# Both expert layers by Strassen's scheme: seven block products for each 2x2 blocks, with sums by VectorE and in PSUM

## The chip, the cores and the metric

One core of a Trainium2 chip runs one program. The metric is the device time of one execution in microseconds (us); three executions are shown as their median. A profiled execution gives the trace on which everything below rests. TensorE (PE; its weight loads are PEld) does matrix products into PSUM, eight banks of 512 float32 a partition; VectorE (DVE), ScalarE (ACT) and GpSimd (POOL) do element-wise work; SyncE (SP) starts most DMAs.

## The reference

Input x is 4 samples x 512 tokens x 256 channels. Two layers of a transformer-like network are computed: modulated attention over heads and a Mamba block, a modulated linear layer and an fp8 linear layer, embeddings with layer norms, attention with 16 heads, and last the part that matters here:

```python
x = x + _L1_ffn_ref(_L1_cond2_ref(x, cond_512, ...), ...)

# _L1_ffn_ref, with xf = x.reshape(-1, 256), E = 8 experts of 512 hidden units
logits = xf @ gate_w.T + gate_b        # RMS-normed, softmax, top-1 value g
norm_g = g / (g + 1e-6)
h = gelu(einsum('nd,edh->neh', xf, w1) + b1)     # exact gelu
y = einsum('neh,ehd->ned', h, w2) + b2
out = (y * norm_g[:, None, None]).sum(axis=1)    # over all eight experts
```

Every token goes through all eight experts, so the experts together are one two-layer network 256 -> 4096 -> 256 in float32.

## The kernel before

The program is one function, `program`, with one instruction stream an engine (`block.tensor`, `block.scalar`, `block.vector`, `block.gpsimd`, `block.sync`), and semaphores between them. Activations lie transposed: channels on the 128 partitions (C = 2 chunks), a sample's 512 tokens along the free dimension. The order on each engine is the order of the code; nothing is planned at run time. The stages follow each other: first attention and Mamba until about 680 us, the linear and embedding layers until about 1000, attention until 1190, and the stage in question from there.

The lead-in (from line 1331): `decoded(b)` computes each sample's 256x256 decoder weights (line 1339), VectorE copies them and the bias (2223, 2226). Between these stand the last steps of attention: `z_rows`, `zn_columns`, `attention_out` (1281) on TensorE, `normalise` (2189, 2191) and `attention_add` (2197) on VectorE. Then the products of line 1365 give y4, the network's input, for sample after sample; ScalarE adds the bias (1791). When all four are there TensorE does the gate: 32 products of 8 columns, 64 records, into bank 6 (1372), whose results VectorE (2235 to 2261) and ScalarE (1794 to 1798) turn into one factor a token.

The experts (`experts`, `hidden`): 4096 hidden units are FM = 32 blocks of 128. For block f of sample b TensorE does two products of 128x128 weights and 512 columns into one of four banks (`hidden`, 1381), ScalarE applies gelu into `hid` (1805), and two steps later TensorE adds two products of that block with w2 into the two banks of the sample's output (1396), which stay open for all 32 blocks:

```python
for f in range(FM + 2):
    if f < FM:
        hidden(b, f)
    ...
    if f >= 2:
        pe.wait_ge(s_hid, b * FM + f - 2 + 5)
```

Samples alternate between output banks 0, 1 and 6, 7 (`turn`). During sample 0 the gate factor is spread over the partitions in bank 7 (1406), four products a sample, and copied into `ngb` (2264). Samples 0 and 1 are written out; samples 2 and 3 are a loop. When a sample's last block is in, VectorE's `finish` adds b2 and multiplies by the factor (2269), adds to xT (2272), and SP sends the sample out (757). GpSimd does nothing in this stage. SP loads w1 and w2 during attention (semaphore s_ew).

## Time and profile before

| | us |
|---|---|
| median of 3 runs | 1680.3 |
| lowest, highest | 1673.84, 1683.36 |
| profiled execution, its own time | 1684.6 |
| its span in the trace | 1682.8 |
| TensorE busy | 1507.3 |
| VectorE busy | 836.5 |
| ScalarE busy | 805.5 |
| GpSimd busy | 477.2 |
| mean granted TensorE clock | 0.949 of 2.4 GHz |

How to read it: the span goes from the first to the last instruction of the trace. A group of instructions is written "line engine op out<-in shapes xcount | busy us, mean ns of one | idle us before it, and what ended most of it". One float32 product stands as two records of weight load and two of matmul; a matmul record's duration contains the passage through the array, so successive records overlap and their spacing, not their duration, is the pace. A timeline line is "start us, length in us, engine, line, operation, xcount [idle before <- what ended it]". A window line gives the window, its length, the busy time and count for PE, PEld, DVE, ACT and POOL, then the granted clock as a share of 2.4 GHz, the DMA share and GB/s.

### The profile page before, as it was taken

How to read it: one execution, taken by the hardware profiler on the slowest of the kernel's cores; microseconds unless marked ns; L12 is line 12 of the kernel's file. 1: busy time of each engine (PE TensorE's matmuls, PEld its weight loads, DVE VectorE, ACT ScalarE, POOL GpSimd, SP SyncE). 2: the span in 40 equal slices, each digit the busy share in tenths (PEclk: the TensorE clock that was granted, in tenths of full speed). 3: DMA queues.
4: the chain of work that ended last, by engine and by line, in shares of the span. 5: the costliest groups of instructions: out<-in, count | busy, mean ns of one | idle time of the engine just before them, and what ended most of it. 6: DMA issues, size and time to landing. Idle time of an engine off the chain costs nothing.

```text
span 1682.8 us, 18326 instructions
## 1 busy us (share of the span) xinstructions
PE 1507.3 (90%) x6640; PEld 848.9 (50%) x6652; DVE 836.5 (50%) x868; ACT 805.5 (48%) x1346; POOL 477.2 (28%) x140
## 2 busy tenths in 40 slices
PE   5888796699999998979998968898999999999998
PEld 3666342488888887534443323332454444444443
DVE  6994676499797978744335656674100000000000
ACT  2432476499797977513331756776311121221121
POOL 0997300099797977003213200000000000000000
PEclk7899899699999999889999989999889999999999
DMA  6100011213222113110121261220000000000000
GB/s 255 63 16 1 0 51 78 113 52 125 90 110 78 51 46 136 36 39 19 57 75 49 88 244 39 57 56 1 1 0 0 1 13 0 13 0 0 13 0 13
DMA packets 35604, 87.47 MB, mean 52 GB/s; under 512 B 8238, under 2 KB 24836, under 8 KB 32836
## 3 DMA queue, kind: packets, MB, share of 16 engines
q1 hardware_dynamic: 35524, 86.39, 15.1%
q8 instruction: 51, 0.84, 0.2%
q14 instruction: 29, 0.24, 0.0%
HBM read 68.10 MB, written 18.21 MB: 51 GB/s over the span
## 4 chain that ended last, share of the span: by engine, by line
PE 55%; ACT 3%; issue 2%; DVE 2%; DMA 1%; DVEq 1%; ACTq 0%
PE ps L1381 13%; PE ps L1396 13%; PE ps L1256 3%; PE ps L1123 3%; PE ps L1298 3%; PE ps L1244 2%; PE ps L1149 2%; PE ps L1085 2%; ACT arena L1765 1%; PE ps L955 1%; DMA arena<-mrow 1%; PE ps L549 1%; PE ps L1281 1%; PE ps L1007 1%; PE ps L1157 1%
## 5 line engine op out<-in xcount | busy, mean ns | idle before, releaser
L2309 POOL TENSOR_TENSOR arena<-arena 128x2048 f32<-128x2048 f32 x63 | 287.3, 4586 | 167.6 <-DVE arena L1953 167.4
L1953 DVE TENSOR_TENSOR_SCAN arena<-arena,ps 128x1024 f32<-128x1024 f32 x128 | 284.2, 2271 | 45.0 <-ACT arena L1608 22.4
L1805 ACT ACTIVATE arena<-ps,arena 128x512 f32<-128x512 f32 x128 | 87.9, 687 | 348.7 <-PE ps L1381 348.7
L1381 PE MATMUL ps<-arena 128*128 128x512 f32 x512 | 241.7, 597 | 0.0
L1396 PE MATMUL ps<-arena 128*128 128x512 f32 x512 | 239.3, 592 | 0.0
L1765 ACT ACTIVATE arena<-ps,rho 128x512 f32<-128x512 f32 x256 | 158.6, 687 | 60.6 <-PE ps L1298 59.6
L1608 ACT ACTIVATE arena<-arena,mam 128x511 f32<-128x511 f32 x256 | 165.9, 709 | 34.4 <-DVE arena L1953 34.4
L2185 DVE TENSOR_REDUCE mxs<-ps 128x1 f32<-128x512 f32 x224 | 141.7, 684 | 61.7 <-PE ps L1244 59.8
L2269 DVE SCALAR_TENSOR_TENSOR arena<-ps,b2s,arena 128x512 f32<-128x512 f32 x8 | 5.6, 746 | 334.4 <-PE ps L1396 334.4
L1381 PEld LDWEIGHTS ps<-arena 128*128 128x128 f32 x512 | 97.9, 192 | 121.4 <-issue 121.2
L1396 PEld LDWEIGHTS ps<-arena 128*128 128x128 f32 x512 | 97.3, 190 | 122.4 <-issue 122.4
L943 PE MATMUL ps<-early,arena 128*128 128x128 f32 x768 | 129.7, 277 | 18.2 <-DVE arena L1953 17.9
L2289 POOL TENSOR_TENSOR arena<-arena 128x4096 f32<-128x4096 f32 x16 | 115.0, 7188 | 44.6 <-DVE arena L1872 44.6
L1596 ACT ACTIVATE arena<-arena,early 128x512 f32<-128x512 f32 x192 | 123.8, 708 | 0.1
L955 PE MATMUL ps<-early,arena 128*128 128x128 f32 x1024 | 121.5, 272 | 0.9 <-POOL arena L2309 0.8
L1298 PE MATMUL ps<-arena 97*128 97x512 bf16 x256 | 98.7, 394 | 18.2 <-DMA arena<-mrow 14.1
L955 PEld LDWEIGHTS ps<-early,arena 128*128 128x128 f32 x1024 | 113.6, 141 | 1.9 <-POOL arena L2309 1.2
L943 PEld LDWEIGHTS ps<-early,arena 128*128 128x128 f32 x768 | 90.6, 142 | 31.8 <-DVE arena L1953 22.9
L944 PE MATMUL ps<-arena 128*128 128x128 f32 x512 | 99.4, 276 | 0.0
L1244 PE MATMUL ps<-arena 96*128 96x512 bf16 x224 | 87.9, 392 | 0.0
L806 PE MATMUL ps<-early,arena 128*128 128x128 f32 x512 | 64.6, 288 | 21.3 <-POOL arena L2289 21.2
L1256 PE MATMUL ps<-arena 128*32 128x512 f32 x512 | 68.5, 607 | 13.2 <-ACT arena L1765 13.2
(311 smaller groups left out, 1868.8 us busy)
## 6 DMA issues: line engine op xcount, KB each, us to landing
arena<-bc_scratch SPq DMA_DIRECT2D x32, 512.0 KB, 3.7
batch_scratch<-arena SPq DMA_DIRECT2D x2, 3072.0 KB, 9.1
arena<-batch_scratch SPq DMA_DIRECT2D x6, 1024.0 KB, 7.1
arena<-q_scratch SPq DMA_DIRECT2D x96, 64.0 KB, 2.1
arena<-k_scratch SPq DMA_DIRECT2D x96, 64.0 KB, 2.1
arena<-in_dec_w SPq DMA_DIRECT2D x1, 3855.0 KB, 16.6
arena<-in_cond SPq DMA_DIRECT2D x1, 3739.5 KB, 11.7
arena<-in_ids SPq DMA_DIRECT2D x4, 768.0 KB, 7.1
```

What stands on the lines that cost most here:

```text
L943: pe.transpose(ps[:, FEED + m, t * P:(t + 1) * P], dub[:, k % 2, t, m * P:(m + 1) * P], ident)
L955: last = pe.matmul(ps[:, t, m * P:(m + 1) * P], state[:, k % SLOTS, m, t * P:(t + 1) * P], ident, start=False, stop=(k % NS == NS - 1 and ...
L1244: pe.matmul(ps[:, (hg + s) % 3, :], q[0:STACK, i, qc * P:(qc + 1) * P], k[0:STACK, i, :], start=True, stop=True).then_inc(s_s_mm, 1)
L1298: pe.matmul(ps[:, 3 + (hg + n) % 3, :], k[0:STACK + 1, i, kc * P:(kc + 1) * P], q[0:STACK + 1, i, :], start=True, stop=True).then_inc(s_t_ ...
L1381: last = pe.matmul(ps[:, 2 + f % 4, :], w1[:, c, f * P:(f + 1) * P], y4[:, b if isinstance(b, int) else bass.ds(b, 1), c, :], start=(c == ...
L1396: last = pe.matmul(ps[:, 6 * turn + o, :], w2[:, f - 2, o * P:(o + 1) * P], hid[:, (f - 2) % 4, :], start=(f == 2), stop=(f == FM + 1))
L1596: act.activation(dub[:, k % 2, t, :], duT[b % 2][:, t, :], ACT.Copy, scale=bt[:, b, t, n:n + 1])
L1608: last = act.activation(decay[:, (2 * k + h) % 3, i, 1:S], dt[b % 2][:, m, 1:S], ACT.Exp, scale=a_neg[:, m * NS + n:m * NS + n + 1])
L1765: act.activation(pt[:, j % 4, i], ps[:, 3 + (hg + n) % 3, :], ACT.Exp, scale=rho[:, 0:1]).then_inc(s_pt, 1)
L1953: dve.tensor_tensor_scan(half, view(decay[:, (2 * k + h) % 3], [[1, 2 * S]]), view(ps[:, FEED + 2 * h, :], [[1, 2 * S]]), 0.0, ALU.mult, A ...
L2185: dve.tensor_reduce(mxs[:, hg % 2, qc, i:i + 1], ps[:, (turn + s) % 3, :], AX, ALU.max).then_inc(s_max, 1)
L2309: pool.tensor_tensor(state[:, k % SLOTS], state[:, k % SLOTS], view(c_rows[:, j % 2, k % G, :], [[0, M], [1, S]]), ALU.mult).then_inc(s_hc, 1)
```

## The change

The hidden layer takes w1 as 2x2 blocks: rows by chunk k of the input, columns by half of the hidden units (16 blocks of 128 each). A sample's y4 is 2x2: chunk by half of the tokens. The four quarters of the hidden layer's output are made from seven block products instead of eight (the form with shared partial sums, after Winograd). The second layer does the same with w2 (half of the hidden units by output chunk) and the quarters of the hidden activations. The weight sums (`w1_s1`, `w1_s2`, `w1_s4`, the same for w2, and one difference written over each weight) are made once by VectorE before the stage, the sums of y4 once a sample (`x_sums`), the sums of the hidden quarters each round.

A round takes two hidden blocks of the lower and two of the upper half: 8 rounds a sample, 32 in all, all written out. TensorE's products have 256 columns. In a round, in this order: A1 (bank 4), B1 (bank 5), C1 (bank 6); three pairs of the second layer for the round before; A2, B2 (added into banks 4 and 5); two pairs of the second layer; B3, C2; two more pairs; two products a pair. ScalarE copies A1 (`first_in`) before A2 is added and applies gelu to the quarters h11, h22, h21, h12, two operations of 256 columns each. VectorE makes part2 (after B1), part3 and h22 (after B2), h21 (after B3), h12 (after C2), then t1, t2 (`t12`), a difference over h12, and t4 (`t34`): nine operations of 512 columns. The second layer's seven sums stay open in banks 0 to 3 for a sample; `quarters` joins them in the first round of the next sample, with eight operations of 256 columns, and `finish` follows in its second round. The gate products are spread over round 0 between the first layer's pairs, into bank 7; the gate's VectorE and ScalarE steps over rounds 1 to 3; the spreading of the factor goes to round 5 of each sample and its copy to round 6. Storage moves to freed places (the decoded weights, t sums and `first_in` into `mam`, the quarters into `hT`, `part2`, `part3`, `ngb`, `moe` into `early` and `diag`).

The diff, cut to its core:

```diff
@@ block.tensor @@
+            def pair(bank, n, weights, x, first, last):
+                b, r = divmod(n, ROUNDS)
+                for i in range(2):
+                    f = 2 * r + i
+                    done = pe.matmul(ps[:, bank, i * S // 2:(i + 1) * S // 2], weights[:, f, :], x,
+                                     start=first and i == 0, stop=last and i == 1, skip_group_check=True)
+                return done
...
+            def both(bank, half, n, weights, x):
+                r = n % ROUNDS
+                for i in range(2):
+                    f = 2 * r + i
+                    done = pe.matmul(ps[:, bank, half * S // 2:(half + 1) * S // 2], weights[:, f, :], x[:, i, :],
+                                     start=(r == 0 and half == 0 and i == 0),
+                                     stop=(r == ROUNDS - 1 and i == 1 and (half == 1 or bank == 1)))
+                return done
...
+            def second(n, chunk):
+                h11, h12, h21, h22 = h_q[n % 2]
+                t1, t2, t4 = h_t[n % 2]
+                begins = n % ROUNDS == 0 and n
+                if chunk == 0:
+                    pe.wait_ge(s_hid, by_act(n, 4))
+                    if begins:
+                        pe.wait_ge(s_sums, at_vector["out0", n])
+                    both(0, 0, n, w2_b[0][0], h11)
+                    both(0, 1, n, w2_b[0][1], h21)
+                    last = both(1, 0, n, w2_s4, h22)
+                elif chunk == 1:
+                    pe.wait_ge(s_sums, at_vector["t12", n])
+                    both(2, 0, n, w2_s1, t1)
+                    last = both(2, 1, n, w2_s2, t2)
+                else:
+                    pe.wait_ge(s_sums, at_vector["t34", n])
+                    both(3, 0, n, w2_b[1][0], h12)
+                    last = both(3, 1, n, w2_b[1][1], t4)
+                last.then_inc(s_e_mm, 1)
...
+            pe.wait_ge(s_y4, B + 1)
+            pe.wait_ge(s_sums, 1)
+            for n in range(B * ROUNDS):
+                b, r = divmod(n, ROUNDS)
+                x11, x12, x21, x22 = (y4[:, b, k, j * S // 2:(j + 1) * S // 2] for k in range(C) for j in range(2))
+                t1, t2, t3, t4 = (y4_t[:, b % 2, j, :] for j in range(4))
+                if n:
+                    pe.wait_ge(s_hid, by_act(n - 1, 2))
+                pair(A_BANK, n, w1_b[0][0], x11, True, True).then_inc(s_h_mm, 1)
+                if n:
+                    pe.wait_ge(s_sums, at_vector["c21", n - 1])
+                pair(B_BANK, n, w1_s2, t2, True, True).then_inc(s_h_mm, 1)
+                if n:
+                    pe.wait_ge(s_sums, at_vector["c12", n - 1])
+                pair(C_BANK, n, w1_s1, t1, True, True).then_inc(s_h_mm, 1)
+                if n:
+                    second(n - 1, 0)
+                else:
+                    gates(0)
+                    gates(1)
+                pe.wait_ge(s_hid, by_act(n, 1))
+                pair(A_BANK, n, w1_b[0][1], x21, False, True).then_inc(s_h_mm, 1)
+                pe.wait_ge(s_sums, at_vector["u2", n])
+                pair(B_BANK, n, w1_b[1][0], t3, False, True).then_inc(s_h_mm, 1)
+                if n:
+                    second(n - 1, 1)
+                else:
+                    gates(2)
+                pe.wait_ge(s_sums, at_vector["u3", n])
+                pair(B_BANK, n, w1_b[1][1], t4, False, True).then_inc(s_h_mm, 1)
+                pe.wait_ge(s_sums, at_vector["c22", n])
+                pair(C_BANK, n, w1_s4, x22, False, True).then_inc(s_h_mm, 1)
+                if n:
+                    second(n - 1, 2)
+                else:
+                    gates(3).then_inc(s_gate_mm, 1)
+                if r == 5:
+                    spread_gates(b)
+            for chunk in range(3):
+                second(B * ROUNDS - 1, chunk)
@@ block.scalar @@
+            def gelu(quarter, src, n, upper):
+                r = n % ROUNDS
+                for i in range(2):
+                    f = upper * W_HALF + 2 * r + i
+                    last = act.activation(quarter[:, i, :], src[:, i, :], ACT.Gelu, bias=wf["b1"][:, f:f + 1])
+                last.then_inc(s_hid, 1)
+            for n in range(B * ROUNDS):
+                h11, h12, h21, h22 = h_q[n % 2]
+                act.wait_ge(s_h_mm, by_pe(n, 1))
+                if n:
+                    act.wait_ge(s_sums, at_vector["c21", n - 1])
+                act.activation(first_in, ps[:, A_BANK, :], ACT.Copy).then_inc(s_hid, 1)
+                if n == 1:
+                    act.wait_ge(s_ng, 1)
+                    act.activation(gs[:, 1, :], gs[:, 0, :], ACT.Ln, scale=1.0 / E, bias=eps32[:, 0:1])
+                    act.drain()
+                    act.activation(gs[:, 1, :], gs[:, 1, :], ACT.Exp, scale=-0.5).then_inc(s_gate_a, 1)
+                    act.preload_act_table_set("gelu_and_others")
+                if n == 2:
+                    act.wait_ge(s_ng, 2)
+                    act.activation(lg[:, :, :], lg[:, :, :], ACT.Exp, scale=2.0).then_inc(s_gate_a, 1)
+                    act.preload_act_table_set("gelu_and_others")
+                act.wait_ge(s_h_mm, by_pe(n, 4))
+                if n >= 2:
+                    act.wait_ge(s_e_mm, second_layer(n - 2, 3))
+                gelu(h11, view(ps[:, A_BANK, :], [[S // 2, 2], [1, S // 2]]), n, 0)
+                act.wait_ge(s_sums, at_vector["c22", n])
+                gelu(h22, h22, n, 1)
+                act.wait_ge(s_sums, at_vector["c21", n])
+                gelu(h21, h21, n, 1)
+                act.wait_ge(s_sums, at_vector["c12", n])
+                gelu(h12, h12, n, 0)
@@ block.vector @@
+            def weight_sum(out, a, b, op):
+                dve.drain()
+                dve.tensor_tensor(out, a, b, op)
+            def x_sums(b):
+                dve.wait_ge(s_y4, b + 2)
+                x11, x12, x21, x22 = (y4[:, b, k, j * S // 2:(j + 1) * S // 2] for k in range(C) for j in range(2))
+                t1, t2, t3, t4 = (y4_t[:, b % 2, j, :] for j in range(4))
+                dve.tensor_tensor(t1, x12, x11, ALU.subtract)
+                dve.tensor_tensor(t3, x22, x12, ALU.subtract)
+                dve.drain()
+                dve.tensor_tensor(t2, x22, t1, ALU.subtract)
+                dve.drain()
+                dve.tensor_tensor(t4, x21, t2, ALU.subtract).then_inc(s_sums, 1)
+            weight_sum(w1_s1, w1_b[1][0], w1_b[1][1], ALU.add)
+            weight_sum(w1_b[1][0], w1_b[0][0], w1_b[1][0], ALU.subtract)
             dve.wait_ge(s_wgt_mm, 1)
             dve.tensor_copy(dbias[:, :, :], ps[:, 4, 0:C * B])
             decoded(0)
             normalise(B * HG - 1, HG - 1)
             decoded(1)
             decoded(2)
+            weight_sum(w1_s2, w1_s1, w1_b[0][0], ALU.subtract)
             attention_add(B - 1, 0)
             decoded(3)
+            weight_sum(w1_s4, w1_b[0][1], w1_s2, ALU.subtract)
             attention_add(B - 1, 1)
+            weight_sum(w2_s1, w2_b[1][0], w2_b[1][1], ALU.add)
+            weight_sum(w2_b[1][0], w2_b[0][0], w2_b[1][0], ALU.subtract)
+            x_sums(0)
+            weight_sum(w2_s2, w2_s1, w2_b[0][0], ALU.subtract)
+            weight_sum(w2_s4, w2_b[0][1], w2_s2, ALU.subtract)
...
+            def quarters(n):
+                low, high = slice(0, S // 2), slice(S // 2, S)
+                dve.wait_ge(s_e_mm, second_layer(n - 1, 2))
+                dve.drain()
+                dve.tensor_copy(part2[:, low], ps[:, 0, low])
+                dve.drain()
+                dve.tensor_tensor(moe[0][:, low], part2[:, low], ps[:, 0, high], ALU.add)
+                dve.tensor_tensor(part2[:, high], part2[:, low], ps[:, 2, high], ALU.add)
+                dve.drain()
+                dve.tensor_tensor(part3[:, low], part2[:, high], ps[:, 2, low], ALU.add)
+                dve.drain()
+                out0 = dve.tensor_tensor(moe[0][:, high], part3[:, low], ps[:, 1, low], ALU.add)
+                out0.then_inc(s_sums, 1)
+                dve.wait_ge(s_e_mm, second_layer(n - 1, 3))
+                dve.tensor_tensor(part3[:, high], part2[:, high], ps[:, 3, low], ALU.add)
+                dve.drain()
+                dve.tensor_tensor(moe[1][:, low], part3[:, high], ps[:, 3, high], ALU.add)
+                dve.tensor_tensor(moe[1][:, high], part3[:, high], ps[:, 2, low], ALU.add).then_inc(s_sums, 1)
+            def finish(b):
+                dve.drain()
                 for o in range(C):
-                    dve.scalar_tensor_tensor(moe[:, o, :], ps[:, 6 * turn + o, :], b2s[:, o:o + 1], ngb[:, tok(b)],
-                                             ALU.add, ALU.mult)
-                dve.drain()
-                dve.tensor_tensor(xT[:, :, tok(b)], xT[:, :, tok(b)], moe, ALU.add).then_inc(s_x4, 1)
-                dve.drain()
-
-            dve.drain()
-            with dve.Fori(0, B // 2) as i:
-                finish(2 * i, 0)
-                finish(2 * i + 1, 1)
+                    dve.scalar_tensor_tensor(moe[o], moe[o], b2s[:, o:o + 1], ngb, ALU.add, ALU.mult)
+                dve.drain()
+                for o in range(C):
+                    last = dve.tensor_tensor(xT[:, o, tok(b)], xT[:, o, tok(b)], moe[o], ALU.add)
+                last.then_inc(s_x4, 1)
+            for n in range(B * ROUNDS):
+                b, r = divmod(n, ROUNDS)
+                h11, h12, h21, h22 = h_q[n % 2]
+                t1, t2, t4 = h_t[n % 2]
+                flat = lambda quarter: view(quarter, [[1, S]])
+                dve.wait_ge(s_h_mm, by_pe(n, 2))
+                dve.wait_ge(s_hid, by_act(n, 1))
+                dve.drain()
+                dve.tensor_tensor(part2, first_in, ps[:, B_BANK, :], ALU.add).then_inc(s_sums, 1)
+                if n == 1:
+                    gate_power()
+                if n == 2:
+                    gate_less_max()
+                if n == 3:
+                    gate_factor()
+                if r == 1 and b:
+                    finish(b - 1)
+                dve.wait_ge(s_h_mm, by_pe(n, 5))
+                dve.tensor_tensor(part3, first_in, ps[:, B_BANK, :], ALU.add).then_inc(s_sums, 1)
+                if n >= 2:
+                    dve.wait_ge(s_e_mm, second_layer(n - 2, 3))
+                dve.drain()
+                dve.tensor_tensor(flat(h22), part3, ps[:, C_BANK, :], ALU.add).then_inc(s_sums, 1)
+                if r == 4 and b < B - 1:
+                    x_sums(b + 1)
+                if r == 6:
+                    dve.wait_ge(s_ngb_mm, b + 1)
+                    dve.tensor_copy(ngb, ps[:, 7, :]).then_inc(s_ngb, 1)
+                dve.wait_ge(s_h_mm, by_pe(n, 6))
+                dve.tensor_tensor(flat(h21), first_in, ps[:, B_BANK, :], ALU.add).then_inc(s_sums, 1)
+                dve.wait_ge(s_h_mm, by_pe(n, 7))
+                dve.tensor_tensor(flat(h12), part2, ps[:, C_BANK, :], ALU.add).then_inc(s_sums, 1)
+                if r == 0 and b:
+                    quarters(n)
+                dve.wait_ge(s_hid, by_act(n, 5))
+                dve.tensor_tensor(flat(t1), flat(h12), flat(h11), ALU.subtract)
+                dve.drain()
+                dve.tensor_tensor(flat(t2), flat(h22), flat(t1), ALU.subtract).then_inc(s_sums, 1)
+                dve.tensor_tensor(flat(h12), flat(h22), flat(h12), ALU.subtract)
+                dve.drain()
+                dve.tensor_tensor(flat(t4), flat(h21), flat(t2), ALU.subtract).then_inc(s_sums, 1)
+            quarters(B * ROUNDS)
+            finish(B - 1)
```

## Rows read from the trace of the kernel before

**Rows 1.** The page's busy time by engine, whole span.
```profile
PE 1507.3 (90%) x6640; PEld 848.9 (50%) x6652; DVE 836.5 (50%) x868; ACT 805.5 (48%) x1346; POOL 477.2 (28%) x140
```

**Rows 2.** Groups of instructions by line from 1100 us on, expert stage.
```profile
L1381 PE MATMUL ps<-arena 128*128 128x512 f32 x512 | 241.7, 597 | 0.0
L1396 PE MATMUL ps<-arena 128*128 128x512 f32 x512 | 239.3, 592 | 0.0
...
L1805 ACT ACTIVATE arena<-ps,arena 128x512 f32<-128x512 f32 x128 | 87.9, 687 | 348.7 <-PE ps L1381 348.7
...
L1406 PE MATMUL ps<-early,gs 128*128 128x128 f32 x32 | 4.2, 275 | 0.0
```

**Rows 3.** Windows, with the granted clock.
```profile
1150.00:1180.00 30.00, 24.07 (x124) 7.32 (x125) 8.82 (x16) 20.44 (x35) 0.00 (x0) 1.00 0.00 1
1210.00:1230.00 20.00, 18.64 (x81) 13.99 (x79) 0.00 (x0) 3.79 (x6) 0.00 (x0) 0.79 0.00 1
1230.00:1250.00 20.00, 20.00 (x44) 9.23 (x45) 3.17 (x12) 6.24 (x10) 0.00 (x0) 0.87 0.00 0
1400.00:1500.00 100.00, 100.00 (x234) 44.28 (x233) 2.63 (x3) 20.36 (x30) 0.00 (x0) 1.00 0.02 6
```

**Rows 4.** Timeline from the decoder's bias to the first expert products.
```profile
1191.27 0.17 DVE L2226 COPY dbias<-ps 128x8 f32<-128x8 f32 x1 [5.26 <-PE ps L1339]
...
1204.11 0.69 DVE L2197 TENSOR_TENSOR xT<-ps,xT 128x512 f32<-128x512 f32 x1 [1.22 <-PE ps L1281]
...
1207.55 1.26 ACT L1791 ACTIVATE arena<-ps,dbias 128x512 f32<-128x512 f32 x2 [11.59 <-PE ps L1365]
...
1219.16 11.52 PEld L1372 LDWEIGHTS ps<-arena 128*128 128x128 f32 x64 [2.18 <-ACT arena L1791]
...
1230.63 7.69 PE L1381 MATMUL ps<-arena 128*128 128x512 f32 x12
...
1233.87 1.28 ACT L1799 ACT_TABLE_LOAD   x1
```

**Rows 5.** Timeline of TensorE, two like places of the expert stage, 64 blocks apart.
```profile
1442.58 1.88 PE L1381 MATMUL ps<-arena 128*128 128x512 f32 x4
...
1662.32 1.88 PE L1381 MATMUL ps<-arena 128*128 128x512 f32 x4
```

**Rows 6.** Timeline of the end.
```profile
1675.19 0.19 PEld L1396 LDWEIGHTS ps<-arena 128*128 128x128 f32 x1 [0.24 <-issue]
1676.37 1.41 DVE L2269 SCALAR_TENSOR_TENSOR arena<-ps,b2s,arena 128x512 f32<-128x512 f32 x2 [107.06 <-PE ps L1396]
1677.94 1.23 DVE L2272 TENSOR_TENSOR xT<-xT,arena 128x1024 f32 x1 [0.16 <-issue]
1679.34 0.57 SPq L757 DMA_DIRECT2D out<-xT  x1
```

**Rows 7.** Timeline of weight loads around the 256-column products of line 1157.
```profile
786.48 0.19 PEld L1157 LDWEIGHTS ps<-arena 128*128 128x128 f32 x1 [0.24 <-issue]
786.90 3.22 PEld L1157 LDWEIGHTS ps<-arena 128*128 128x128 f32 x15 [0.24 <-issue]
790.15 4.84 PEld L1085 LDWEIGHTS ps<-arena 128*128 128x128 bf16 x23
```

**Rows 8.** Groups by shape, whole span: the 128-column products of line 955.
```profile
L955 PE MATMUL ps<-early,arena 128*128 128x128 f32 x1024 | 121.5, 272 | 0.9 <-POOL arena L2309 0.8 <-DVE arena L2113 0.2
```

**Rows 9.** Groups by shape, whole span, VectorE.
```profile
L1926 DVE TENSOR_TENSOR arena<-arena 128x2048 f32<-128x2048 f32 x4 | 9.2, 2293 | 0.4
...
L2191 DVE TENSOR_TENSOR hT<-ps,zrec 128x256 f32<-128x256 f32 x16 | 6.8, 425 | 1.2
...
L1819 DVE TENSOR_TENSOR arena<-early 128x512 f32<-128x512 f32 x1 | 0.7, 693 | 4.0 <-DMA early<-in_early 4.0
```

**Rows 10.** Groups by shape, whole span, ScalarE on 256 columns.
```profile
L1494 ACT ACTIVATE arena<-arena 128x256 f32<-128x256 f32 x16 | 6.5, 409 | 5.5 <-DVE arena L1861 5.5
```

**Rows 11.** Timeline inside the attention stage: a product that waited for ScalarE.
```profile
1175.70 1.06 PE L1256 MATMUL ps<-arena 128*32 128x512 f32 x8 [1.14 <-ACT arena L1765]
```

More of the change, by code:

```diff
@@ L1367, in _, with gates @@
                 last.then_inc(s_y4_mm, 1)
-            pe.wait_ge(s_y4, B + 1)
-            for b in range(B):
+            def gates(b):
                 for t in range(TILES):
                     for c in range(C):
-                        last = pe.matmul(ps[:, 6, (b * TILES + t) * E:(b * TILES + t + 1) * E],
+                        last = pe.matmul(ps[:, 7, (b * TILES + t) * E:(b * TILES + t + 1) * E],
                                          y4[:, b, c, t * P:(t + 1) * P], gate_w[:, c, :],
@@ L1374, in _ @@
                                          start=(c == 0), stop=(c == C - 1))
-            last.then_inc(s_gate_mm, 1)
-            def hidden(b, f):
-                pe.wait_ge(s_hid, b * FM + f + 1)
-                for c in range(C):
-                    last = pe.matmul(ps[:, 2 + f % 4, :], w1[:, c, f * P:(f + 1) * P],
-                                     y4[:, b if isinstance(b, int) else bass.ds(b, 1), c, :],
-                                     start=(c == 0), stop=(c == C - 1))
-                last.then_inc(s_h_mm, 1)
@@ L1410, in _ @@
[L1410 to L1416 removed]
+                return last
+            def pair(bank, n, weights, x, first, last):
[5 more added lines that the diff above has]
+                return done
@@ new lines, in spread_gates @@
+            def spread_gates(b):
+                pe.wait_ge(s_ng, 3)
+                pe.wait_ge(s_ngb, b)
+                for t in range(TILES):
+                    col = b * TILES + t
+                    last = pe.matmul(ps[:, 7, t * P:(t + 1) * P], gs[:, 3, col:col + 1].to_broadcast([P, P]),
+                                     ident, start=True, stop=True)
+                last.then_inc(s_ngb_mm, 1)
+            pe.wait_ge(s_y4, B + 1)
[36 more added lines that the diff above has]
+                    spread_gates(b)
```

142 lines of the change are left out of this document (63 added, 79 removed).

## The prediction, before the change was built

> **What bounds the kernel now.** I began with the busy time by engine: TensorE works 90% of the span, VectorE and ScalarE about half of it [rows 1]. A share over the whole span says little of one stage, so I went to the groups by line. The two lines of the expert layers, 1381 and 1396, hold 481.0 us of TensorE's time with nothing idle before them, while ScalarE's gelu in the same stage works 87.9 us and waits 348.7 us for TensorE [rows 2]. Each product of 512 columns stands there as two records, so 1024 records are 512 products. The windows say the same of the middle of the stage: in 100 us TensorE is busy 100.00, VectorE 2.63, ScalarE 20.36, and the granted clock is 1.00, the 2.4 GHz level [rows 3]. The timeline gives the stage its ends: gate products from 1219.16, expert products from 1230.63 [rows 4]. In between all goes at one pace: two like places lie 219.74 us and 512 records apart, 0.4292 us a record [rows 5]. The last weight load is at 1675.19; its record takes the next slot and leaves it at 1676.05, and VectorE's closing sums start 0.32 us later [rows 6]. So the stage is 445.4 us of pure TensorE, of which 1024 x 0.4292 = 439.5 are the products; the other 5.9 are the gate-spreading products (4.2 us busy, [rows 2]) and a start at the lower clock. A change pays here exactly what it takes from TensorE's queue, as long as that queue never waits.
>
> **What is removed and added on TensorE.** Four samples of 32 blocks are worked as 32 rounds of four blocks. A round was 16 products of 512 columns, 32 records; it becomes 14 per layer, 28 products of 256 columns, 56 records. In columns that is 7/8. Whether time follows depends on the spacing at 256 columns. The expert stage has no such product, but line 1157 does, same types, other weights each time: weight loads from 786.90 to the first load of the next line at 790.15 make 3.25 us for 15, 0.2167 us a record, with loads of 0.19 us [rows 7]. The loads thus fit behind the product before. Sum: 1792 x 0.2167 = 388.3 us, against 439.5: **51.2 us saved**. The bounds: half of today's record, 0.2146, would give 384.6 (3.7 us better). At 128 columns line 955 takes 121.5 us for 1024 records, 0.1187 each [rows 8]; twice that, 0.2373, gives 425.2 (37 us worse). I take line 1157, the same width.
>
> The load is the thing to weigh: 0.19 of 0.2167 us is nearly the whole slot. The Trainium skill (TensorE: Matmul & The Clock Gate, Back-to-back issue gap) says that in a stream of load and matmul pairs both set the spacing, and that short matmuls come out slower than columns over clock, 81 against 56 ns at 128 columns. By that the halved width would lose part of its gain; by the record of line 955 that loss is small here, 0.1187 us where half of line 1157's record would be 0.1084.
>
> **Can the two other engines keep up?** VectorE goes from nothing to nine 512-column operations a round: 0.69 us each, from PSUM [rows 4] or SBUF [rows 9], 6.2 us, with gaps of 0.08 some 6.8. ScalarE does one copy (at most 0.69, the gelu of 512 columns [rows 2]) and eight gelus of 256 columns; the nearest row is 0.41 us [rows 10], say 0.45: 4.3 us. The round on TensorE is 56 x 0.2167 = 12.14 us, so neither is the bound by volume. What can bite is the order. I lay out a round from its first product, a pair of products being 0.87 us, a consumer starting 0.3 us after a slot ends (rounded from [rows 6]):
> A1 to 0.87, B1 to 1.73, C1 to 2.60, three second-layer pairs of the round before to 5.20, A2 to 6.07, B2 to 6.94, two pairs to 8.67, B3 to 9.54, C2 to 10.40, two pairs to 12.14.
> VectorE: part3 after B2, 7.24 to 7.93, c22 to 8.70. B3 needs the first at 8.67 and C2 the second at 9.54: 0.7 and 0.8 us spare, the tightest places. Then h21 to 10.53, h12 to 11.39. ScalarE is through h12 by about 12.3, the t sums follow to 13.8 and 15.3 (which is 3.1 into the next round). Of those the second layer needs t12 at 19.1 and t34 at 22.5, the gelus (11.4) at 14.7. The next part2 is then ready at 3.9, B2 wants it at 6.07. So in an ordinary round nothing waits. The x sums (four of 256 columns, 0.42 each by [rows 9]) and the spread factor's copy fall into the 1.1 us before B3's result or push h21 by 0.7 us, still 3 us early. I cost these at nothing; their cover is TensorE's own queue of second-layer pairs.
>
> **The three sample ends** are different. After h12 come eight adds and copies of 256 columns: out0 at 13.8 (needed at 14.7), out1 at 15.2, the t sums at 16.6 and 18.1, part2 of the next round at 18.8, where B2 wants it at 18.2: TensorE waits 0.7 us. Then two scaled sums and two adds of 512 columns (0.70 and 0.69 each, 3.0 us in all) stand before part3, which comes at 22.6 against B3's 21.5: 1.1 us more. That is 1.8 us, three times **5.4 us**; bounds nothing and twice that.
>
> **The start.** The weight sums, 2048 columns, 2.29 us each [rows 9], go into VectorE's gaps: two (4.6 us) before the bias copy, which had 5.26 us idle ahead of it; the third and fourth before the attention adds, of which the last moves from 1204.11 to some 1205.3, where the product that needs it is 8 us off; two more and the x sums until about 1213, since the first sample's y4 is ready at 1208.8; the last two until 1218. TensorE starts its first round at 1219.16 as before, when the last y4 is there [rows 4]: nothing. The 32 gate products (64 records, 11.5 us) stay, spread over round 0, where they cover the first waits. What moves is the clock: those 8-column products leave it at 0.79, and after them today's first twelve records take 7.69 us instead of 5.3, at the 1.2 GHz level [rows 3, 4]. Now round 0's 28 records (6.1 us) lie between gate products, so the lower clock can cost from 0 to 6.1 plus today's 2.5. I take 4.0, **1.5 us more**. The gate's ScalarE steps carry two table loads of 1.28 [rows 4] in each of two rounds, in the 4 us in which ScalarE waits for A2, and end before c22 is there; VectorE's gate steps (at most five of 0.3) follow part2 in rounds 1 to 3, from 3.9 to 5.4, before part3's 7.2: nothing. The samples are now all written out where two of four were a loop; the written-out first sample shows no idle time before its products either [rows 2], so nothing for fetching. The output transfers of samples 0 to 2 move a round back on SP, and nobody waits for them.
>
> **The end.** Now 3.1 us lie between the last slot and the output transfer's sums [rows 6]. Then: the first five of the output sums start under the last two pairs and end 0.9 us after the slot, three more take 1.3, the scaled sums and adds 3.0: 5.3 us, **2.2 more**. The transfer itself is the same size.
>
> **The sum**, against the profiled execution (span 1682.8, time 1684.6): -51.2 + 5.4 + 1.5 + 2.2 = -42.1, so 1642.5. The median shown is 1680.3, 4.3 below that execution, and the runs spread over 9.5; a new median should lie by it, so the forecast is **1638 us**. Over or under 0.5%, about 8 us, is what a measurement of this kernel can tell from no change.
>
> **The rivals.**
> *The loop slips in every round (chance 0.16).* The spare at B3 and C2 is 0.7 us; with slower semaphore hand-overs or gaps than I put, each round loses 0.6: 32 x 0.6 = 20 us, 1658. For: two tight places in each round, two dependent PSUM reads. Against: the gaps here come from rows.
> *Nothing waits (0.09).* Sample ends hidden, clock as today, spacing 0.2146: 3.7 + 5.4 + 1.5 = 10.6 off, 1628.
> *Weight loads show (0.05).* By the 128-column row, 37 us back: 1675, no change that can be told. For: 88% of the slot is load. Against: line 1157 runs exactly this. This is the way the Trainium skill's section on the issue gap, named above, would have it go.
> *Slower (0.05): the clock falls.* If TensorE's waits at B3 bring it to 1.2 GHz, a round costs up to 12.1 us more; from 42.1/12.1 = 3.5 such rounds on the gain is gone. If every round waits 0.8 us and then takes today's 2.5 us to recover, 3.3 x 32 = 106 us more: 1744. Against: in the attention stage TensorE waited 1.14 us for ScalarE, the window was only 80% busy, and the clock stayed at 1.00 [rows 3, 11].
> My own forecast has the remaining 0.65.
>
> **Numbers.** Forecast 1638; range 1628 to 1660, which takes in the first two rivals and the bounds of the sample ends and leaves out the last two (0.10) and some of the slipping loop. Faster by over 0.5%: 0.65 + 0.16 + 0.09 = 0.90; within: 0.05; slower: 0.05.
>
> **What would show it.** TensorE's weight loads in the expert stage 0.217 us apart; rounds 12.1 us long; the stage's end near 1632 in the trace; VectorE at about 55% there, ScalarE at 35%; waits of TensorE for VectorE only in rounds 8 and 9, 16 and 17, 24 and 25. Wrong would be: spacing above 0.225 with no wait named (loads), a wait before every B3 or C2 (loop), a granted clock below 0.95 from 1260 on (clock), VectorE's 512-column sums over 0.8 us.

## The result and the profile after

| | before | after |
|---|---|---|
| median, us | 1681.83 (4 runs) | 1635.14 (4 runs) |
| lowest, highest | 1673.84, 1685.69 | 1632.79, 1637.53 |
| profiled execution, its span | 1684.6, 1682.8 | 1633.2, 1631.4 |
| forecast | | 1638 (1628 to 1660) |

The measured ratio is 0.9728, with a 95% interval from 0.9688 to 0.9769. The medians differ by 46.7 us where 42.1 were forecast, the spans of the two profiled executions by 51.4. I read the new trace in the order of the forecast's steps. First the page's busy time by engine and the groups from 1180 us on (columns as in [rows 1, 2]):

```profile
PE 1454.8 (89%) x7408; PEld 994.1 (61%) x7420; DVE 1067.1 (65%) x1216; ACT 855.9 (52%) x1511; POOL 477.4 (29%) x140
```

```profile
L1412 PE MATMUL ps<-arena 128*128 128x256 f32 x896 | 215.5, 387 | 3.3 <-DVE early L2439 1.9 <-ACT arena L1870 1.4
...
L1421 PE MATMUL ps<-hT,arena 128*128 128x256 f32 x512 | 121.2, 380 | 0.0
...
L1421 PE MATMUL ps<-mam,arena 128*128 128x256 f32 x384 | 93.3, 379 | 0.0
L1878 ACT ACTIVATE hT<-hT,arena 128x256 f32<-128x256 f32 x192 | 85.7, 502 | 86.4 <-DVE hT L2443 54.9 <-DVE hT L2450 30.7 <-DVE hT L2452 0.8
...
L2456 DVE TENSOR_TENSOR mam<-hT 128x512 f32<-128x512 f32 x32 | 22.1, 692 | 28.9 <-ACT hT L1878 28.9
...
L2439 DVE TENSOR_TENSOR early<-mam,ps 128x512 f32<-128x512 f32 x32 | 22.0, 687 | 101.1 <-PE ps L1412 101.1
```

The 896 records of line 1412 and the 512 and 384 of line 1421 are the 1792 that were counted. With the 1024 of the kernel before [rows 2] they account for the whole difference in TensorE's number of records, 7408 against 6640 [rows 1]. VectorE's 512-column sums take 0.69 us, as priced. ScalarE's 256-column gelu takes 0.50 from SBUF where I had said 0.45; nothing follows from it, since ScalarE sits idle before it.

The windows, first the new trace's (columns as in [rows 3]), then two of the trace of before for the same times:

```profile
1180.00:1195.00 15.00, 13.14 (x68) 5.95 (x67) 9.67 (x13) 7.57 (x13) 0.00 (x0) 1.00 0.00 1
1195.00:1210.00 15.00, 14.11 (x35) 6.32 (x34) 14.43 (x13) 3.78 (x6) 0.00 (x0) 1.00 0.01 1
1210.00:1230.00 20.00, 18.64 (x88) 15.68 (x87) 4.51 (x6) 5.99 (x12) 0.00 (x0) 0.77 0.00 1
1230.00:1250.00 20.00, 20.00 (x80) 17.40 (x81) 9.70 (x17) 10.96 (x18) 0.00 (x0) 0.80 0.00 0
...
1300.00:1600.00 300.00, 298.09 (x1387) 260.82 (x1386) 168.38 (x264) 99.61 (x218) 0.00 (x0) 1.00 0.02 6
```

```profile
1180.00:1195.00 15.00, 13.14 (x70) 5.88 (x62) 2.90 (x9) 7.97 (x14) 0.00 (x0) 0.86 0.01 2
1195.00:1210.00 15.00, 15.00 (x33) 6.67 (x32) 2.77 (x5) 1.86 (x3) 0.00 (x0) 0.80 0.00 0
```

From 1300 to 1600 TensorE works 298.1 of 300 us at the 2.4 GHz level, VectorE 56%, ScalarE 33%: the forecast said 55 and 35. What TensorE misses there are the sample ends. They show in the timeline of weight loads, here the first of the three, with the ordinary round after it:

```profile
1332.49 2.56 PEld L1412 LDWEIGHTS ps<-arena 128*128 128x128 f32 x12
...
1338.93 0.73 PEld L1412 LDWEIGHTS ps<-arena 128*128 128x128 f32 x4 [0.42 <-DVE early L2429]
...
1342.40 1.59 PEld L1412 LDWEIGHTS ps<-arena 128*128 128x128 f32 x8 [1.02 <-DVE early L2439]
...
1345.75 2.56 PEld L1412 LDWEIGHTS ps<-arena 128*128 128x128 f32 x12
...
1357.84 2.56 PEld L1412 LDWEIGHTS ps<-arena 128*128 128x128 f32 x12
```

A round begins with twelve loads of line 1412 (A1, B1, C1). The ordinary one goes from 1345.75 to 1357.84, **12.09 us** (forecast 12.14), or 0.2159 a record. The one with the sample's end goes from 1332.49 to 1345.75, 13.26, so **1.17 us** more. The two waits that were named are the only ones, 0.42 us for line 2429 (part2) and 1.02 for 2439 (part3). Both lie in the next sample's second round; in its first, which the forecast's signs had allowed too, none shows.

The lead-in and the start, from the timeline; the last three lines are of the trace of before:

```profile
1189.35 0.17 DVE L2343 COPY dbias<-ps 128x8 f32<-128x8 f32 x1 [0.42 <-PE ps L1370]
...
1196.47 1.96 PE L1312 MATMUL ps<-hT,arena 128*128 128x512 f32 x4 [0.89 <-DVE xT L2297]
1213.51 2.46 PEld L1412 LDWEIGHTS ps<-arena 128*128 128x128 f32 x12 [2.19 <-ACT arena L1870]
...
1221.62 3.75 PEld L1402 LDWEIGHTS ps<-arena 128*128 128x128 f32 x16
...
1236.98 3.07 PEld L1421 LDWEIGHTS ps<-hT,arena 128*128 128x128 f32 x12
...
1237.41 3.05 PE L1421 MATMUL ps<-hT,arena 128*128 128x256 f32 x12
...
1240.30 1.89 PE L1412 MATMUL ps<-arena 128*128 128x256 f32 x8
```

```profile
1197.26 3.78 PE L1281 MATMUL ps<-hT,arena 128*128 128x512 f32 x4
...
1201.08 0.69 DVE L2197 TENSOR_TENSOR xT<-ps,xT 128x512 f32<-128x512 f32 x1 [3.02 <-PE ps L1281]
...
1238.16 1.88 PE L1396 MATMUL ps<-arena 128*128 128x512 f32 x4
```

And the end:

```profile
1621.86 0.84 PEld L1421 LDWEIGHTS ps<-mam,arena 128*128 128x128 f32 x4
...
1627.07 0.68 DVE L2418 TENSOR_TENSOR xT<-xT,diag 128x512 f32<-128x512 f32 x1
1627.93 0.57 SPq L788 DMA_DIRECT2D out<-xT  x1
```

The sum, step by step, against the forecast's; the stage is counted from the first product after y4 to the end of the span:

| step | forecast | profile | how |
|---|---|---|---|
| products | -51.2 | -52.6 | 1792 x 0.2159 = 386.9 against 439.5 |
| sample ends | +5.4 | +3.5 | 3 x 1.17 |
| start | +1.5 | +1.7 | see below |
| end | +2.2 | +1.7 | last slot 1622.94, last add ends 1627.75: 4.8 against 3.1 |
| sum | -42.1 | -45.7 | |
| stage, read directly | | -45.7 | 463.6 (1219.16 to 1682.8) to 417.9 (1213.51 to 1631.4) |
| ahead of the stage | 0 | -5.7 | 1219.16 to 1213.51 |

For the start I go by the starts of products. From 1213.51 to the first second-layer product of round 1, at 1237.41, are 23.9 us, and the lower clock costs another 0.3 behind that (those twelve records take 2.89 us, to 1240.30, where 12 x 0.2159 make 2.59). Less the 40 expert records in it (8.6) that is 15.6. Before, the gate products took from 1219.16 to 1230.63, 11.5 us, and the first twelve expert records from there to 1238.16, 7.5 where 12 x 0.4292 make 5.15, so 2.4 too long: 13.9 in all.

The last line was in no sum of the forecast. The windows show the granted clock at 1.00 from 1180 to 1210 where the trace of before has 0.86 and 0.80, and 3.7 of those 5.7 us lie between the bias copy and the first product after y4: 24.2 us (1189.35 to 1213.51) against 27.9 [rows 4]. The other 2.0 lie earlier and were not followed up. How far the 3.7 go by execution is looked at in experiment 8.

### The profile page after: what moved, and what is told of

Same layout as the page of the kernel before. It is cut to its first block, busy times and chain, and to the rows that moved or that the text cites. A ratio compares the mean times of both kernels' runs of the same rounds, so it can differ in the third digit from the quotient of the medians.

```text
span 1631.4 us, 20342 instructions
## 1 busy us (share of the span) xinstructions
PE 1454.8 (89%) x7408; PEld 994.1 (61%) x7420; DVE 1067.1 (65%) x1216; ACT 855.9 (52%) x1511; POOL 477.4 (29%) x140
## 3 DMA queue, kind: packets, MB, share of 16 engines
q1 hardware_dynamic: 35524, 86.39, 15.7%
## 4 chain that ended last, share of the span: by engine, by line
PE 53%; ACT 3%; DVE 2%; issue 2%; DMA 1%; DVEq 1%; ACTq 0%
PE ps L1412 12%; PE ps L1421 12%; PE ps L1287 4%; PE ps L1154 3%; PE ps L1329 3%; PE ps L1275 2%; PE ps L1180 2%; PE ps L1116 2%; ACT arena L1845 2%; PE ps L986 1%; DMA arena<-mrow 1%; PE ps L580 1%; PE ps L1312 1%; PE ps L1038 1%; PE ps L1188 1%
## 5 line engine op out<-in xcount | busy, mean ns | idle before, releaser
L1412 PE MATMUL ps<-arena 128*128 128x256 f32 x896 | 215.5, 387 | 3.3 <-DVE early L2439 1.9
L1412 PEld LDWEIGHTS ps<-arena 128*128 128x128 f32 x896 | 172.2, 193 | 30.0 <-DVE early L2439 3.1
L974 PE MATMUL ps<-early,arena 128*128 128x128 f32 x768 | 129.7, 277 | 18.3 <-DVE arena L2053 17.9
L1878 ACT ACTIVATE hT<-hT,arena 128x256 f32<-128x256 f32 x192 | 85.7, 502 | 86.4 <-DVE hT L2443 54.9
L986 PE MATMUL ps<-early,arena 128*128 128x128 f32 x1024 | 121.5, 272 | 0.9 <-POOL arena L2494 0.7
L1421 PE MATMUL ps<-hT,arena 128*128 128x256 f32 x512 | 121.2, 380 | 0.0
L1421 PEld LDWEIGHTS ps<-hT,arena 128*128 128x128 f32 x512 | 97.7, 191 | 13.4
L1878 ACT ACTIVATE hT<-ps,arena 128x256 f32<-128x256 f32 x64 | 26.9, 471 | 138.9 <-PE ps L1412 138.9
L1421 PE MATMUL ps<-mam,arena 128*128 128x256 f32 x384 | 93.3, 379 | 0.0
L2439 DVE TENSOR_TENSOR early<-mam,ps 128x512 f32<-128x512 f32 x32 | 22.0, 687 | 101.1 <-PE ps L1412 101.1
```

The lines of the kernel that those rows point to most:

```text
L974: pe.transpose(ps[:, FEED + m, t * P:(t + 1) * P], dub[:, k % 2, t, m * P:(m + 1) * P], ident)
L986: last = pe.matmul(ps[:, t, m * P:(m + 1) * P], state[:, k % SLOTS, m, t * P:(t + 1) * P], ident, start=False, stop=(k % NS == NS - 1 and ...
L1412: done = pe.matmul(ps[:, bank, i * S // 2:(i + 1) * S // 2], weights[:, f, :], x, start=first and i == 0, stop=last and i == 1, skip_group ...
L1421: done = pe.matmul(ps[:, bank, half * S // 2:(half + 1) * S // 2], weights[:, f, :], x[:, i, :], start=(r == 0 and half == 0 and i == 0), ...
```

## The experiments

The total of one kernel spreads over 5 to 21 us between executions, and goes with the mean granted clock (in experiment 2 from 1671.9 us at 0.959 to 1689.8 at 0.949). So I read each trace at the same places: **start**, from the first product after y4 to the first second-layer weight load of round 1, and **rest**, from there to the end of the span. The changed kernel has 23.5 and 394.4; 0.5 of the 394.4 is the lower clock, which reached into the first twelve loads (3.07 us for 2.56). The ratio beside each is against the kernel before, from runs on the same chip.

**1. 256 columns without the scheme.** The kernel before, each product in two halves.

```diff
-last = pe.matmul(ps[:, 2 + f % 4, :], w1[:, c, f * P:(f + 1) * P], y4[:, ..., c, :], ...)
+for h in range(2):
+    part = slice(h * S // 2, (h + 1) * S // 2)
+    last = pe.matmul(ps[:, 2 + f % 4, part], w1[:, c, f * P:(f + 1) * P], y4[:, ..., c, part], ...)
```
and the same for w2.

> The kernel before, with every expert product of 512 columns made as two of 256 (2048 records instead of 1024, no scheme). Theory (columns alone set the time, weight loads hide behind 256 columns): spacing 0.216 us a record, 2048 x 0.2159 = 442 against 439.5 us, so +3 us, no change that can be told. Rival (weight loads show at 256 columns, by the 128-column record of line 955): spacing 0.237, 486 us, +46 us.

Measured: ratio 1.0000 (0.9972 to 1.0029); the stage took 466.2 us (1211.25 to 1677.4), +2.6. Weight loads in mid-stage, from the timeline:

```profile
1501.27 1.70 PEld L1383 LDWEIGHTS ps<-arena 128*128 128x128 f32 x8
...
1508.17 1.70 PEld L1383 LDWEIGHTS ps<-arena 128*128 128x128 f32 x8
```

Between the two, 32 loads: 6.90 us, 0.2156 each. Doubling the number of loads and products costs 0.6% of the stage. The rival of 0.237 is out. This was the term on which most of the forecast hung, and it had come from 16 records of another stage [rows 7].

**2. Eight products in the changed kernel.**

```diff
+pair(A_BANK, n, w1_b[0][1], x21, False, False)
 pair(A_BANK, n, w1_b[0][1], x21, False, True).then_inc(s_h_mm, 1)
 ...
 both(3, 0, n, w2_b[1][0], h12)
+both(3, 0, n, w2_b[1][0], h12)
```

> The changed kernel with one pair of products more in each layer of each round, 32 products of 256 columns instead of 28, so as many columns as before the change, with all sums kept. It adds products, so its output is another. Theory (TensorE's queue is the round): 32 x 8 records x 0.2159 = +55 us on the changed kernel, about 1690, some 8 us slower than before the change. Rival (rounds are set by hand-overs between engines): part of the added products falls into waits, under +45 us.

Measured: 1679.4 us, ratio 0.9983 (0.9948 to 1.0019): the scheme with an eighth product is where the kernel before is. Rest 444.3, +49.9 on the changed kernel. The expectation was some 5 too high, and by my own reading: 252 added records lie in the rest, 54.4 us, but with longer rounds TensorE no longer waits at the sample ends (the trace has no wait of its loads for VectorE), which gives 3.5 back: 50.9. The 1690 also carried the changed kernel's long start (23.5), where this trace has 19.9; what else parts it from the median of 1679.4 one trace can't tell. The gain of the change is the missing product; that nothing else in it costs in an ordinary round, experiment 5 shows more directly.

**3 and 4. One or two more VectorE operations ahead of part3.**

```diff
 dve.wait_ge(s_h_mm, by_pe(n, 5))
+dve.tensor_tensor(part3, first_in, first_in, ALU.add)
+dve.drain()
```

> The changed kernel with one more VectorE operation of 512 columns (and its drain, 0.77 us) in each round ahead of part3. The trace of the changed kernel shows 0.57 us between the end of part3 and the weight load of B3. Theory (one tight place, priced by its own spare): 0.2 us late in each of 32 rounds, +6 us, with waits of B3's loads for VectorE. Rival (VectorE is 56% busy, so 0.77 us fits in a round of 12.1): +0.

> As the run before, with two more operations (1.54 us a round). Theory: 0.97 us late in each of 32 rounds, +31 us. Rival of free room by busy share: +0. Second rival (the waits bring TensorE's clock down to 1.2 GHz): over +100 us, granted clock below 0.95 in the stage.

Measured: one: ratio 0.9715 (0.9648 to 0.9782), rest 399.3, **+4.9**; two: 0.9895 (0.9841 to 0.9948), rest 423.0, **+28.6**. The waits of the first run (engine, line <- whom, us in total, times, longest) and two successive loads of its B3; then the same loads and the window of the second run:

```profile
PEld ps L1412 <- DVE early L2441: 11.6, 31, 1.8
```

```profile
1345.04 1.59 PEld L1412 LDWEIGHTS ps<-arena 128*128 128x128 f32 x8 [0.22 <-DVE early L2441]
...
1357.22 1.59 PEld L1412 LDWEIGHTS ps<-arena 128*128 128x128 f32 x8 [0.22 <-DVE early L2441]
```

```profile
1314.55 1.59 PEld L1412 LDWEIGHTS ps<-arena 128*128 128x128 f32 x8 [0.99 <-DVE early L2443]
...
1317.90 2.56 PEld L1412 LDWEIGHTS ps<-arena 128*128 128x128 f32 x12
...
1327.49 1.59 PEld L1412 LDWEIGHTS ps<-arena 128*128 128x128 f32 x8 [0.99 <-DVE early L2443]
```

```profile
1300.00:1600.00 300.00, 281.41 (x1285) 239.91 (x1285) 191.05 (x297) 93.23 (x205) 0.00 (x0) 1.00 0.02 6
```

With one more sum an ordinary round is 12.18 us (1345.04 to 1357.22), +0.09; with two it is 12.94 (1314.55 to 1327.49), +0.85. In the changed kernel VectorE is idle for 5.3 us of a round (44% of 12.09), and yet 1.54 more cost 29 us: the spare that counts is the one at that place. The rule by busy share fails. The second rival fails as well: the loads of B3 wait 1 us in each round, TensorE is idle for 6% of the window, and the clock stays at 1.00, which was read before from the attention stage [rows 11] and now holds here.

**5. The sums nearly taken away.**

```diff
-dve.tensor_tensor(part2, first_in, ps[:, B_BANK, :], ALU.add).then_inc(s_sums, 1)
+dve.tensor_tensor(part2[:, some], first_in[:, some], ps[:, B_BANK, some], ALU.add).then_inc(s_sums, 1)
```
with `some` the first 64 columns, and so for all nine.

> The changed kernel with VectorE's nine sums of each round made on 64 of 512 columns, the rest left out (so its output is another); products, gelus and order as they are. Theory (the sums are hidden but for the three sample ends, where TensorE waits some 1.2 us each): -3.5 us. Rival (sums cost something in every round): -10 us or more.

Measured: ratio 0.9689 (0.9655 to 0.9723), rest 390.4, **-4.0**; the trace has no wait of the loads for VectorE. So all 32 x 9 sums together cost the changed kernel 3.5 us (the other 0.5 is the clock in the changed kernel's rest), and that is the price of its three sample ends, 3 x 1.17. Its start took 15.7 us, with the granted clock at 1.00 throughout, though its round 0 has the same products in the same order:

```profile
1207.81 2.46 PEld L1412 LDWEIGHTS ps<-arena 128*128 128x128 f32 x12 [2.19 <-ACT arena L1870]
...
1215.59 1.97 PEld L1402 LDWEIGHTS ps<-arena 128*128 128x128 f32 x16
...
1223.48 2.56 PEld L1421 LDWEIGHTS ps<-hT,arena 128*128 128x128 f32 x12
...
1223.69 2.75 PE L1421 MATMUL ps<-hT,arena 128*128 128x256 f32 x12
```

Sixteen loads for the gate take 1.97 us here; at the lower level they had taken 3.75. The short sums are not the reason for the full clock, as far as the totals can tell: the profiled execution took 1615.6 us at a mean clock of 0.961, the other six 1629.1 to 1632.7 at 0.947 to 0.950, about where the changed kernel lies.

**6. finish one round later.**

```diff
-if r == 1 and b:
+if r == 2 and b:
     finish(b - 1)
```

> The changed kernel with finish of a sample in the next sample's third round instead of its second, all else equal. Theory (of the 1.2 us that a sample end costs, 0.8 is B3 waiting for part3 behind finish): -2.3 us, the waits for line 2439 gone, those for part2 (0.4 us each) left. Rival (the wait only moves to the third round): 0.

Measured: ratio 0.9683 (0.9642 to 0.9724), rest 391.3, **-3.1**, of which 0.5 is again the lower clock in the other's rest: -2.6 for the -2.3 expected. The waits for part3 are gone, those for part2 left, 0.4 us each:

```profile
PEld ps L1412 <- DVE early L2429: 1.3, 3, 0.4
```

**7. The gate's products: all first, or one sample a round.** All ahead of round 0 (first diff), and, on top of 6, one sample in each of rounds 0 to 3 (second). Both diffs are cut: with the second the gate's ScalarE and VectorE steps move to rounds 4 to 6, the spreading of the factor to round 7 and its copy to the next sample's second round.

```diff
 pe.wait_ge(s_sums, 1)
+for b in range(B):
+    last = gates(b)
+last.then_inc(s_gate_mm, 1)
```
```diff
 if n:
     second(n - 1, 1)
-else:
-    gates(2)
+if n < B:
+    last = gates(n)
```

> The changed kernel with all 32 gate products ahead of round 0, as before the change. Theory (in round 0 they cover waits of TensorE for the two other engines, so that spreading them gives back what the clock costs): the 12.5 us that round 0 takes above its own columns become 11.5 for the gates, 3 of open waits and less time at the lower clock: +1 to +3 us. Rival (spreading them only lengthens the time at the lower clock): -2 to -5 us.

> As the run before, and the gate's 32 small products one sample each in rounds 0 to 3 instead of all in round 0, the gate's other steps in rounds 4 to 6, the spreading of the factor in round 7. Theory (the run of small products in round 0 holds TensorE at 1.2 GHz from about 1220 to 1237, which costs some 8 us): the granted clock stays at 1.00, the start is about 5.5 us shorter, -7.8 us on the changed kernel with the 2.3 of finish. Rival (the clock falls whatever the order): -2.3 us.

Measured, all first: ratio 0.9719 (0.9682 to 0.9755), start 21.7, rest 393.9. With no gate products in round 0 to cover it, TensorE's load for B3 waits 1.18 us for part3 there, once. The start lies between the starts that the changed kernel's own round 0 has had (15.7 to 24.0 with the next experiment), so this comparison is inconclusive.

One sample a round: ratio 0.9666 (0.9627 to 0.9706), median 1624.1 us against experiment 6's 1631.2, the stage 407.0 us against 417.9, the clock at 1.00 all through. But the profiled execution, at 1617.7, was the fastest of its six, and one of them took 1634.8. One profile at full clock could be luck, as in 5, so it was run again.

**8. Again, side by side.** The changed kernel; the version of 7 with two weight sums moved behind the attention adds; the kernel before.

```diff
-weight_sum(w1_s2, w1_s1, w1_b[0][0], ALU.subtract)
 attention_add(B - 1, 0)
 decoded(3)
-weight_sum(w1_s4, w1_b[0][1], w1_s2, ALU.subtract)
+weight_sum(w1_s2, w1_s1, w1_b[0][0], ALU.subtract)
 attention_add(B - 1, 1)
+weight_sum(w1_s4, w1_b[0][1], w1_s2, ALU.subtract)
```

> The changed kernel once more, beside the next run on the same chip. In five profiles with the changed kernel's round 0, the stretch from the first product of round 0 to round 1's second-layer pairs took between 15.7 and 23.7 us by how long the clock stood at its lower level. Theory (chance of each execution): it takes again something between 15.7 and 24, the rest of the stage, from there to the end of the span, 394 us as before. Rival (the length goes with the kernel's text): 23.5 us again.

> Gate products over rounds 0 to 3 and finish in the third round, as run before; and the third weight sum behind the first attention add, the fourth behind the second, where TensorE waited 0.9 us for that add in the trace of the changed kernel. Theory: granted clock 1.00 from round 0 on again; lead-in 0.9 us shorter when it runs at full clock; stage from round 0 to the end of the span 407 us; 7 to 9 us under the changed kernel's median. Rival (the full clock of that one profile was luck): the stage within 2 us of the changed kernel's less 2.5.

> The kernel before once more, for the clock in the lead-in: in its first trace the stretch from the bias copy to the first gate product took 27.9 us, in the changed kernel's 24.2. Theory (the clock there goes by execution, not by the change): the stretch lies anywhere from 24 to 28, the expert stage from the first gate product to the end of the span at 463.6 +-1. Rival (the change shortened it): 27.9 again.

Measured: the changed kernel 1632.03, ratio 0.9693 (0.9658 to 0.9727), start 24.0, rest 393.9, stage 417.9; the version 1622.64, ratio **0.9644** (0.9611 to 0.9676), stage 406.9. The windows of the version:

```profile
1195.00:1210.00 15.00, 15.00 (x32) 6.53 (x31) 9.83 (x8) 1.27 (x2) 0.00 (x0) 0.81 0.00 0
1210.00:1230.00 20.00, 18.64 (x78) 13.29 (x77) 13.50 (x15) 9.68 (x17) 0.00 (x0) 1.00 0.00 1
1230.00:1250.00 20.00, 20.00 (x109) 17.98 (x107) 8.91 (x14) 5.86 (x13) 0.00 (x0) 1.00 0.00 0
...
1300.00:1600.00 300.00, 299.96 (x1400) 263.41 (x1399) 172.37 (x270) 101.87 (x223) 0.00 (x0) 1.00 0.02 6
```

and the changed kernel's again:

```profile
1195.00:1210.00 15.00, 14.11 (x40) 6.58 (x39) 13.41 (x13) 2.04 (x4) 0.00 (x0) 1.00 0.00 0
1210.00:1230.00 20.00, 18.64 (x83) 13.81 (x81) 7.40 (x7) 7.26 (x12) 0.00 (x0) 0.87 0.00 1
1230.00:1250.00 20.00, 20.00 (x76) 17.34 (x76) 7.87 (x14) 8.53 (x14) 0.00 (x0) 0.70 0.00 0
```

With sixteen gate records a round over four rounds the clock stood at 1.00 from 1210 on in both profiles, and here the profiled execution was the slowest of its six, so it was no lucky one. With all 64 in round 0, also between full products, the clock fell in six of seven (starts of 17.4, 17.4, 23.5, 23.7 and 24.0 us, and 19.9 with the eighth product; only experiment 5's, 15.7, kept it). Two of two against one of seven makes it likely that the spreading does it, and does not prove it. The size fits: of the 11.0 us by which the stage is shorter (406.9 against 417.9), the start at full clock makes 24.0 - 15.7 = 8.3 and experiment 6's finish 2.6.

How long round 0 stays at the lower level seems to go with what the clock did just before, in these seven: where the lead-in too had run partly at the lower level (26.5, 27.8 and 29.8 us from bias copy to first product) the starts were 17.4, 19.9 and 17.4; where it had run at full clock (24.2) they were 23.5, 23.7, 24.0 and 15.7. Seven are few, and nothing here tests why.

The version is the fastest measured here: 9.4 us under the changed kernel on the same chip, 60 under the kernel before.

The kernel before, again: stage 463.7 us (1218.45 to 1682.1); from bias copy to y4 26.5 us, not 27.9. The version had 26.5 too, with the clock at 0.81 from 1195 to 1210, and the changed kernel 24.2 again. The changed kernel's lead-in, with the same products, took from 24.2 to 29.8 us by its clock, so a difference of 3.7 between two executions shows nothing of the change. That the kernel before would reach 24.2 as well isn't shown: in none of its three traces (26.5 in experiment 1's, too) was the clock at 1.00 throughout there. The move of the weight sums can't be judged: in that trace the lead-in ran at the lower clock, where VectorE was idle 3.0 us ahead of the add anyway.

## Why the prediction was right

**Products.** Right and the heart of it. 0.2167 us a record was taken, 0.2159 measured, which is 1.4 of the 3.6 us by which the stage came out better than its steps (-45.7 for -42.1). The bound from the 128-column row was never near. The Trainium skill (TensorE: Matmul & The Clock Gate, Back-to-back issue gap) holds that the pair of load and matmul sets the spacing and short matmuls lose by it; at 256 columns of float32, with loads of 0.19 us in slots of 0.216, the runs show next to none of that: 0.5% between half and whole products in experiment 1.

**Two other engines keep up.** Right. In an ordinary round nothing waits; the spare at B3 was put at 0.7, and the prices of experiments 3 and 4 give just that: 0.77 us more made a round 0.09 longer, 1.54 made it 0.85 longer, so 0.68 and 0.69 were free. (The 0.57 in the expectations had been read at the weight load, which runs ahead of its product.) VectorE starts 0.20 us after a slot's end, not 0.3; here B2's last slot ends where the next product starts:

```profile
1364.96 1.89 PE L1421 MATMUL ps<-mam,arena 128*128 128x256 f32 x8
...
1365.16 0.69 DVE L2439 TENSOR_TENSOR early<-mam,ps 128x512 f32<-128x512 f32 x1 [3.36 <-PE ps L1412]
```

The gap of 0.08 us between two sums stood in no row of the forecast, though the forecast says that its gaps come from rows; the new trace has 0.07 to 0.09.

**Sample ends.** The mechanism and both places right, the size 1.17 for 1.8. The shorter hand-over fits the difference in part; no run takes it apart. Experiment 5 shows it as the whole price of the sums, and 6 takes the larger part away.

**Start.** The size right (1.7 for 1.5), but by luck. I gave 4.0 us to the lower clock where it had cost 2.5. Experiment 5's round 0, at full clock, takes 15.9 us to its first second-layer product (1207.81 to 1223.69), 7.2 above its 40 records; the 15.6 and 13.9 above therefore hold 8.3 and 6.6 us of lower clock. The gate products themselves were slower at the lower level (11.5 us before), and I had counted that as their fixed price. Both costs were too small by 4, and only their difference came out. And it is no fixed number: with the same products in round 0 the start took from 15.7 to 24 us.

**Lead-in.** The third weight sum (2.29 us) was costed at nothing, in the 3.02 us that VectorE was idle ahead of the first attention add (the line at 1201.08 above; no row of the forecast has it). In the new trace TensorE waits 0.89 us for that add at 1196.47, and so in all six traces with the lead-in at full clock. The idle time had been measured while TensorE was at its lower clock: the four products ahead of the add took 3.78 us then, where four such take 1.96 at full clock. They came sooner, and the weight sum stood in the way. Idle time that is to cover an edit, read at one clock, isn't there at the other. What lies ahead of the stage came out 5.7 us shorter all the same in this pair of traces. 3.7 of it goes with the clock, and no step had it; the medians, 46.7 us apart, hold little of it.

**End.** 1.7 for 2.2, by the same shorter hand-over.

**Rivals.** The loop that slips in every round did not come; experiment 4 shows that it would have from 0.7 us on, at about 33 us for each further microsecond in a round. "Nothing waits" failed by the sample ends, and "weight loads show" by experiment 1. The clock as the way to a slower kernel fell with experiment 4.

## What to carry to other kernels

Where one engine's queue is the stage, a scheme that trades products for sums is worth its products, as long as each sum lands before the place in the queue that needs it; here 52.6 us of products came at 6.9 of sample ends, start and end. Find the smallest of these spares, since the engine's free time says nothing about it. Price a new operand width from any stage that has it. Try spreading a lump of small products thinly, a few in each round, where the clock falls over them. And before you put an edit into another engine's idle time, ask whether that time was read at the lower clock, and what is left of it at full clock.

## What the runs showed of the hardware

Some things I had not expected. A wait of the weight loads of about 1 us in each 13 us round, with TensorE idle for 6% of the time, left its clock at 1.00 over 300 us (experiment 4). And in round 0 of the changed kernel, where TensorE was never idle but had the 64 records of 8-column products among its work, the clock went to the 1.2 GHz level for 17 us, by execution for shorter (3 us in experiments 3 and 6) or not at all (experiment 5):

```profile
1221.00:1238.00 17.00, 17.00 (x58) 14.85 (x57) 7.17 (x13) 5.60 (x11) 0.00 (x0) 0.50 0.00 1
```

Further, a weight load that comes 0.19 us late delays the products by half of that: with one more sum the loads waited for VectorE in 31 rounds, yet an ordinary round grew from 12.09 to 12.18 us only. The loads run ahead of their products in every trace here, which would explain it. A 256-column gelu on ScalarE took 0.50 us from SBUF, 0.47 from PSUM, where the exponential of the same width had taken 0.41 [rows 10].
